# Putting a table of row sums together ahead of the last three row additions: a graph layer and a 64-expert layer on one core

## The reference

```python
x = x + gnn(layernorm(x), edges, ...)
n = layernorm(x)
shared = sum(swiglu(n, sWg[e], sWu[e], sWd[e]) for e in range(2))
gate = top-6 softmax weights, zero elsewhere        # 625 x 64
routed = sum(swiglu(n, Wg[e], Wu[e], Wd[e]) * gate[:, e:e+1] for e in range(64))
out = x + shared + routed + n
```

## Time and profile before

| | |
|---|---|
| median of 3 runs | 756.45 us (755.75 to 759.19) |
| the profiled execution's own time | 754.59 us |
| its span, first to last instruction | 752.8 us |
| PE, share of the span busy | 93% |
| DVE, ACT, POOL | 33%, 29%, 23% |
| DMA traffic over the span | 236.33 MB, mean 314 GB/s |

### The profile page before, as it was taken

The page is one execution under the profiler, slowest core; times in us unless marked ns, Lnnn a source line. Parts: engine busy times, 40 slices in busy tenths (PEclk is TensorE's granted clock), DMA queues, the critical chain, the costliest instruction groups (busy, mean ns, idle before and its releaser), DMA issues. The chain is left out here.

```text
span 752.8 us, 17410 instructions
## 1 busy us (share of the span) xinstructions
PE 696.7 (93%) x6982; PEld 474.1 (63%) x6982; DVE 251.4 (33%) x795; ACT 221.1 (29%) x536; POOL 174.0 (23%) x157
## 2 busy tenths in 40 slices
PE   3689999899999999999999999999999999999960
PEld 2467777566766666555666666655567777777740
DVE  6975625775112432221212111122323222221000
ACT  5733323512332222212222222221222333233320
POOL 4000000012222322323322222223333332232202
PEclk9999999999999999999999999999999999999996
DMA  9925112447999999999999999999999999999962
GB/s 270 410 86 224 39 74 81 156 145 261 362 372 343 388 389 382 386 393 385 378 389 383 381 399 380 385 393 385 385 382 375 371 368 370 367 375 373 381 165 28
DMA packets 63408, 236.33 MB, mean 314 GB/s; under 512 B 7323, under 2 KB 7359, under 8 KB 51550
## 3 DMA queue, kind: packets, MB, share of 16 engines
q1 hardware_dynamic: 51764, 211.33, 73.3%
q0 software_dynamic: 10144, 20.56, 11.7%
q10 hardware_dynamic: 1418, 3.30, 1.2%
HBM read 222.32 MB, written 12.83 MB: 312 GB/s over the span
## 5 line engine op out<-in xcount | busy, mean ns | idle before, releaser
L461 POOL DMA_INDIRECT xg<-x_tab,idx_sb x64 | 69.9, 1092 | 375.5 <-DVE idx_sb L1048 193.6
L1528 PE MATMUL ps<-ring,xT 128*64 128x256 f32 x1296 | 148.4, 380 | 0.2 <-DVE hs L1107 0.2
L473 POOL DMA_INDIRECT out<-ysb,idx_sb x64 | 93.3, 1458 | 189.6 <-issue 112.7
L1528 PEld LDWEIGHTS ps<-ring,xT 128*64 128x64 f32 x1296 | 93.6, 137 | 46.7 <-issue 1.1
L1041 DVE TENSOR_REDUCE gates<-ps 128x1 f32<-128x3 f32 (+1 forms) x62 | 10.0, 162 | 331.3 <-PE ps L1434 330.6
L707 ACT ACTIVATE ysb<-ps 64x256 f32<-64x256 f32 x64 | 24.1, 377 | 201.4 <-PE ps L1528 192.9
L1528 PE MATMUL ps<-ring,hTj 128*64 128x256 f32 x624 | 76.0, 386 | 0.0
L1528 PE MATMUL ps<-w,xT 128*64 128x256 f32 x608 | 69.8, 379 | 0.4 <-DMA w<-in_L_ffn_Wu 0.4
L1009 DVE TENSOR_TENSOR onehot<-iotaAB,slotv 125x640 bf16<-125x640 f32 (+1 forms) x64 | 67.3, 1052 | 0.5 <-issue 0.3
L1528 PEld LDWEIGHTS ps<-ring,hTj 128*64 128x64 f32 x624 | 41.4, 136 | 28.7 <-issue 11.7
L1528 PEld LDWEIGHTS ps<-w,xT 128*64 128x64 f32 x608 | 44.3, 137 | 22.0 <-issue 0.8
(11 more groups left out here) (254 smaller groups left out, 819.2 us busy)
## 6 DMA issues: line engine op xcount, KB each, us to landing
ring<-in_L_ffn_Wd SPq DMA_DIRECT2D x39, 1024.0 KB, 18.5
ring<-in_L_ffn_Wg SPq DMA_DIRECT2D x27, 1024.0 KB, 19.3
ring<-in_L_ffn_Wu SPq DMA_DIRECT2D x27, 1024.0 KB, 17.6
w<-in_L_ffn_Wd SPq DMA_DIRECT2D x20, 1024.0 KB, 21.7
w<-in_L_ffn_Wg SPq DMA_DIRECT2D x14, 1024.0 KB, 14.9
ring<-in_L_ffn_Wg SPq DMA_DIRECT2D x28, 512.0 KB, 15.1
w<-in_L_ffn_Wu SPq DMA_DIRECT2D x13, 1024.0 KB, 20.4
ring<-in_L_ffn_Wu SPq DMA_DIRECT2D x26, 512.0 KB, 16.3
```

The lines of the kernel that those rows point to most:

```text
L461: g.indirect_dma_start(out=xg[j % NX][0:ROWS[j], :], out_offset=None, in_=x_tab, in_offset=bass.IndirectOffsetOnAxis(ap=idx_sb[0:ROWS[j], ...
L473: g.indirect_dma_start(out=out, out_offset=bass.IndirectOffsetOnAxis(ap=idx_sb[0:ROWS[j], j:j + 1].bitcast(u32), axis=0), in_=ysb[j % NY][ ...
L1528: last = t_.matmul(ps[h * BIG:(h + 1) * BIG, bank, 0:AW], big(k), w[:, k, h * AW:(h + 1) * AW], start=(k == 0), stop=(k == KD - 1))
```

## The change

All additions up to position 60 (`MERGE_AFTER`) go into a second internal table `y_tab`, which is zeroed in place of `out`. After scatter 60 has landed, SP loads the table into a new SBUF buffer `fin` (it lies where `xnT` was), tile by tile, in two parts each, with a semaphore per tile. GpSimd waits for each tile, adds `x_sb` to it with a `tensor_tensor`, and SP stores the tile plainly into `out`. Scatter 61 waits for all ten stores, and 61, 62 and 63 are added into `out` as before. The waits and DMAs of the merge stand on SP's queue behind the last ring load and ahead of the overflow branch, and on GpSimd's queue between scatters 60 and 61.

```diff
-    BASE_AFTER = 59
+    MERGE_AFTER = 60
...
+        rHT.rewind()
+        fin = rHT.place("fin", [P, T, D], f32)
...
+        y_tab = nc.dram_tensor("y_tab", [N, D], f32, kind="Internal").ap()
...
-        s_base = sem("base_added")
+        s_fin = [sem(f"sum_in{t}") for t in range(T)]
+        s_merged, s_out = sem("merged"), sem("out_written")
...
+            rows_of = out.rearrange("(t p) d -> p t d", p=P)
+            sums_of = y_tab.rearrange("(t p) d -> p t d", p=P)
+            sp.wait_ge(s_sy, NS * T)
+            sp.wait_ge(s_scat, 16 * (MERGE_AFTER + 1))
+            for t in range(T):
+                for a, b in PARTS:
+                    sp.dma_start(fin[a:b, t, :], sums_of[a:b, t, :]).then_inc(s_fin[t], 16)
+            for t in range(T):
+                sp.wait_ge(s_merged, t + 1)
+                for a, b in PARTS:
+                    sp.dma_start(rows_of[a:b, t, :], fin[a:b, t, :]).then_inc(s_out, 16)
             sp.wait_ge(s_ov, 1)
...
-            sp.wait_ge(s_base, 32)
+            sp.wait_ge(s_out, 32 * T)
...
-            g.dma_start(out[0:full * 128, :].rearrange("(t p) d -> p t d", p=128),
+            g.dma_start(y_tab[0:full * 128, :].rearrange("(t p) d -> p t d", p=128),
                         zrows[:].unsqueeze(1).broadcast_to([128, full, D])).then_inc(s_pre, 16)
-            g.dma_start(out[full * 128:rest, :], zrows[0:EVEN, :]).then_inc(s_pre, 16)
-            g.dma_start(out[rest:N, :], zrows[0:N - rest, :]).then_inc(s_pre, 16)
+            g.dma_start(y_tab[full * 128:rest, :], zrows[0:EVEN, :]).then_inc(s_pre, 16)
+            g.dma_start(y_tab[rest:N, :], zrows[0:N - rest, :]).then_inc(s_pre, 16)
...
-                if j == BASE_AFTER + 1:
-                    pool.wait_ge(s_base, 32)
+                if j == MERGE_AFTER + 1:
+                    pool.wait_ge(s_out, 32 * T)
                 pool.sem_inc(s_go, 1)
-                g.indirect_dma_start(out=out,
+                g.indirect_dma_start(out=y_tab if j <= MERGE_AFTER else out,
...
-            def add_base():
+            def merge():
                 pool.wait_ge(s_sy, NS * T)
-                pool.wait_ge(s_scat, 16 * (BASE_AFTER + 1))
-                for a, b in PARTS:
-                    g.dma_start(out.rearrange("(t p) d -> p t d", p=P)[a:b, :, :], x_sb[a:b, :, :],
-                                accum_op=ALU.add).then_inc(s_base, 16)
+                for t in range(T):
+                    pool.wait_ge(s_fin[t], 32)
+                    g.tensor_tensor(fin[:, t, :], fin[:, t, :], x_sb[:, t, :], ALU.add).then_inc(s_merged, 1)
...
-                if j == BASE_AFTER:
-                    for i in range(n, min(E, n + 1)):
+                if j == MERGE_AFTER:
+                    for i in range(n, E):
                         gather(i)
-                    n = min(E, n + 1)
-                    add_base()
+                    n = E
+                    merge()
```

More of the change, by code:

```diff
@@ L339, in gnn_moe_kernel @@
         AFTER = min(j for j in unit_at if j > SPREAD + 5)
-        assert max(unit_at) < BASE_AFTER
+        assert max(unit_at) < MERGE_AFTER
         DT = 3
```

## The result

The changed kernel took 768.44 us in the median (4 runs, 766.03 to 768.95) against 757.62 for the kernel before (4 runs): ratio 1.0145, 95% interval 1.0125 to 1.0165. It is slower by about 1.5%, outside my range. The profiled execution took 768.95 us with a span of 766.9.

What follows compares the result with a forecast made beforehand. The base's landing and four additions in a row were taken to set the end. Three additions instead (5.3 us gained), from a point 2.5 us later, gave 2.8 us less: 753.65 us (-0.37%), range 749.2 to 758.8.

Steps and rivals of the forecast that it cites:

- step 4: Loads of y_tab on SP's queue: 0.81 us per tile plus 2.0 to land, first tile in SBUF at 724.0.
- step 7: Additions 61 to 63 and close: two intervals of 5.29 us plus 5.89 for the last, 16.47 us, end at 750.0.
- What bounds the kernel: End of the kernel: set by the base's landing plus four additions in a row, 21.75 us from the base on.
- Step 1: Zeroing y_tab instead of out and sending 61 additions there: same work, costed at nothing.
- Step 2: Position 60's addition no longer waits for the base: goes out at 712.5, lands at 721.2 (bounds 717.3 and 721.9).
- Step 3: Last weights land at about 721 instead of 726.8, queues empty at 720.8; PE's 3.73 us stall goes, worth nothing itself.
- rival D: The weights' slow end isn't the base's doing: 61 starts near 738.5, end 2.2 us later, 758.7; chance 0.05.
- Step 5: Five GpSimd additions of the merge at 1.17 us each, 5.85 us in all, the last done at 729.9.
- Rival B: GpSimd's merge additions are slower: at 3.0 us each the kernel takes 6.4 us more, 762.8; chance 0.09.
- Step 6: Stores of merged tiles: 0.81 us issue, 2.0 landing, 0.85 to the next start; position 61 starts at 733.5.
- the signs that the prediction ends with: Signs of being wrong: additions over 1.9 us or delayed, tiles landing over 4 us, 61 to 63 awaiting y, changes before 703.

Runs made afterwards that it cites:

- e4: The kernel before with the base's addition taken out, so its output lacks the base; 755.26 us, ratio 0.9979.
- k1: The g1 kernel with SP's loads of the table held back until the last y is ready; 768.23 us (one run).
- h1: The g1 kernel with the ten loads of the table issued by ACT in place of SP; 760.33 us, ratio 1.0038.
- e1: The changed kernel with the five additions of the merge moved from GpSimd to DVE; 766.61 us, ratio 1.0118.
- g1: The changed kernel with one small plain DMA more on GpSimd's queue, behind position 60's addition and ahead of the merge; 759.83 us, ratio 1.0037.
- e2: The kernel before with one 125x512 f32 GpSimd addition into a spare buffer, right behind the base's two additions; 757.36 us, ratio 1.0001.
- e3: The kernel before with one 64x64 f32 GpSimd addition near the start, ahead of GpSimd's first DMA; 757.20 us, ratio 1.0004.

## Why the prediction was wrong

I forecast 2.8 us less; the profiled spans differ by 14.1 us the other way. Two terms of the sum failed, the landing of the loads in step 4 and the kernel's close in step 7. By my steps:

- **What bounds the kernel** held: the chain of the last additions sets the end, and 61 to 63 never waited for y or weights.
- **Step 1**, the start: nothing moved there.
- **Step 2**, position 60: issued behind 59 as forecast, landed at 719.5 on before's scale (723.60 less 4.14), where I had 721.2: 1.7 us sooner.
- **Step 3**, the last weights: PE's stall for them went, as forecast; the down weights of position 62 had landed by 722.3 on before's scale, where before they took until 726.8. But that the queues then are empty at 720.8 was wrong: the last weight landed at 726.9. I spread 3.01 MB evenly over all engines at 384 GB/s; e4 shows the share falling to 0.69 and 0.37 over 8 us with no base at all. My rival D had named this, with 61 at 738.5 (measured 737.7), and I gave it 0.05.
- **Step 4**, the loads, is the term of the merge that failed: 8.30 us to the first tile instead of 2.81, +5.5. The size I took is right for empty queues (3.04 in k1). A tile needs all the parts of its two transfers, and a second queue (h1) doesn't bring the late ones sooner. That it is the engines still busy with weights that are late is what h1, k1 and the spread of the landing events leave; which engines these are, the trace doesn't say.
- **Step 5**, the additions: 6.15 us for five where I had 5.85. Each took 1.26 us where four times the affine select gave 1.17. The estimate from the Trainium skill ("GPSIMD Engine Reference", section on elementwise cycle accounting), 1.12, was low by 0.14. Rival B was not the cause: with DVE in GpSimd's place (e1) position 61 gained 0.9 us.
- **Step 6**, the stores: 3.81 us from the last addition to position 61, forecast 3.66. Steps 2 to 6 together: 61 at 737.7 instead of 733.5.
- **Step 7**: the two intervals were 4.65 and 4.81, together 1.1 us less than twice my mean. The 6.22 that I had averaged in is, by the reading above, the clearing at the 129th DMA, which the changed kernel never reaches: that this came out in its favour was luck. The last term failed: I took over 5.89 us for the last addition with the kernel's close, and it was 15.58. The base's two plain DMAs, which I counted only as a transfer that goes away, also kept GpSimd's DRAIN short. g1 shows it: one plain DMA of 8 KB back on the queue, the DRAIN is 0.885 us, and the kernel is 0.4% slower than before, not 1.5%.
- The sum: +4.2 (steps 2 to 6), -1.1 (intervals), +9.7 (close) on -2.8 gives +10.0, and 4.1 is the quick execution of before; by the medians the difference is 10.8.

Of the signs that the prediction ends with, one did show: tiles landing over 4 us after their issue. None was about the close; I took the 5.89 us from the trace as one piece and didn't ask what it was made of.

## What to carry to other kernels

Read the stretch behind the last addition too: a kernel's close has its own price, and here it depended on which DMAs GpSimd had issued. Whoever takes the last plain DMA off GpSimd's queue, in a kernel with some 128 or more DMAs there, should look at GpSimd's DRAIN and try a small one in its place. And a transfer that must pass through all DMA engines lands when the slowest is through with its backlog, so don't price a load at the end of a heavy stream by bytes over mean rate; look at the share of busy engines in that stretch.

## What the runs showed of the hardware

- GpSimd's closing DRAIN took 10.52 us in the four kernels with 128 DMAs from the first gather on and none of them plain, and 0.885 to 4.89 us in all the others. All lengths fit 0.068 us plus 0.0817 for each entry left, counted as in the table. An addition more on GpSimd, or five fewer, changed nothing (e1, e2, e3).
- With 129 or more DMAs from the first gather on, one addition, the 129th, went out late: 2.9 us in g1, 1.7 in g2, 1.4 in the kernel before.
- A 125x512 f32 addition took 1.26 us on GpSimd with its operands in SBUF; the one in e2, issued right behind two DMAs, took 2.06. Five of them on DVE took 3.10 us in e1.
- The accumulating base of 1.28 MB took 14.0 and 16.7 us in the midst of the weights, 9.4 and 10.4 at their end, 9.5 and 10.3 behind it.
- At the end of the stream of weights the DMA engines finished unevenly: a share of 0.69 and then 0.37 for 8 us (e4), and 12.4 us between the first and the last landing event of one 1 MB transfer in the changed kernel.
